# One masked eviction per score tile, a third score buffer and an undeferred unit tail in an attention stage

## The reference

```python
xn = _layernorm(x)
Q, K, V = heads(xn @ Wq + bq), heads(xn @ Wk + bk), heads(xn @ Wv + bv)   # 16 heads of 64
scores = einsum('bhsd,bhtd->bhst', Q, K) / sqrt(64)
mask = where(i - j >= 0, 0.99 ** (i - j), 0.0)          # query i, key j
retained = einsum('bhst,bhtd->bhsd', scores * mask, V)
attn = (layernorm(retained) * gamma + beta) * sigmoid(xn @ Wg + bg) @ Wo + bo
ffn = sum over 8 experts of weight_e * (gelu(xn @ W1_e + b1_e) @ W2_e + b2_e)
out = x + attn + ffn
```

## Time and profile before

| | us |
|---|---|
| runs shown: median of 3 (lowest to highest) | 13451.64 (12078.26 to 13509.96) |
| the profiled execution | 12024.38 |
| its span, slowest core (core 1) | 12022.8 |
| spans of the other seven cores | 12004.4 to 12017.8 |
| mean granted clock by core | 0.843 to 0.849 |

### The profile page before, as it was taken

How to read it: one execution, slowest core, us unless ns; L and a number is a source line. 1 busy time by engine, 2 the same in 40 slices (tenths; PEclk the granted TensorE clock), 3 DMA queues, 4 the chain that set the end, 5 groups by cost and what they waited for, 6 DMA issues and landing times.

```text
span 12022.8 us, 105462 instructions; the slowest of 8 cores (12004.4 to 12022.8 us)
## 1 busy us (share of the span) xinstructions
PE 9491.4 (79%) x39485; PEld 3786.1 (31%) x39485; DVE 5122.3 (43%) x6656; ACT 1631.5 (14%) x1573; POOL 2.3 (0%) x7
## 2 busy tenths in 40 slices
PE   0376762699999999999947776269999999999995
PEld 0111111343343443444411111134444444444442
DVE  4255552344444444444424555334444444444443
ACT  2200001211111111111100000021111111111111
POOL 0000000000000000000000000000000000000000
PEclk7655556899999999999976555579999999999997
DMA  1100001122222222222220000111112211111112
GB/s 42 32 7 7 6 7 27 56 70 70 70 70 70 70 70 71 70 71 70 70 70 8 7 7 7 28 42 70 71 63 77 71 70 70 71 70 70 71 70 70
DMA packets 334567, 636.28 MB, mean 53 GB/s; under 512 B 75460, under 2 KB 125164, under 8 KB 334070
## 3 DMA queue, kind: packets, MB, share of 16 engines
q1 hardware_dynamic: 319862, 578.94, 14.2%
q10 hardware_dynamic: 14208, 50.60, 1.2%
HBM read 612.72 MB, written 16.78 MB: 52 GB/s over the span
## 4 chain that ended last, share of the span: by engine, by line
PE 72%; DVE 12%; DMA 7%; issue 4%; ACT 4%; DVEq 1%; ACTq 0%; SPq 0%
PE ps_h L1304 30%; PE ps_o L1353 29%; PE ps_s L717 4%; PE ps_r L768 3%; DVE st_buf L746 2%; DVE st_buf L751 2%; ACT L1330 1%; ACT hb L1330 1%; PE ps_qk L683 1%; DMA wqk_st<-wk 1%; DVE st_buf L757 1%; PE ps_g L1062 1%; PE ps_v L539 1%; PE ps_o L1136 1%; DMA xo<-x 1%
## 5 line engine op out<-in xcount | busy, mean ns | idle before, releaser
L1376 DVE SCALAR_TENSOR_TENSOR acc<-ps_o,wrt,acc 128x1024 f16<-128x1024 f32 x2048 | 2628.9, 1284 | 4036.3 <-PE ps_o L1353 3963.5
L1304 PE MATMUL ps_h<-xn_t,w1c 128*128 128x512 bf16 x16384 | 3640.3, 385 | 379.8 <-ACT hb L1330 332.3
L1353 PE MATMUL ps_o<-w2c,hb 128*128 128x512 bf16 x16384 | 3601.2, 378 | 8.0 <-DVE acc L1376 5.1
L1304 PEld LDWEIGHTS ps_h<-xn_t,w1c 128*128 128x128 bf16 x16384 | 1613.0, 99 | 2401.1 <-issue 548.1
L1353 PEld LDWEIGHTS ps_o<-w2c,hb 128*128 128x128 bf16 x16384 | 1475.6, 97 | 2111.0 <-issue 590.5
L1330 ACT ACTIVATE hb<-ps_h,b1t 128x1024 bf16<-128x1024 f32 x1024 | 1127.1, 1113 | 1918.6 <-PE ps_h L1304 1917.1
L717 PE MATMUL ps_s<-qp,kp 64*128 64x512 bf16 x1280 | 756.4, 593 | 457.7 <-DVE st_buf L746 198.6
L768 PE MATMUL ps_r<-st_buf,Vt 128*64 128x512 bf16 x1280 | 805.2, 629 | 56.5 <-DVE st_buf L746 54.8
L1330 ACT ACT_TABLE_LOAD x128 | 164.2, 1283 | 4427.0 <-PE ps_o L1353 4291.6
L736 DVE TENSOR_SCALAR st_buf<-ps_s,ckcols 128x512 bf16<-128x512 f32 x768 | 576.3, 750 | 193.6 <-PE ps_s L717 161.0
L717 PEld LDWEIGHTS ps_s<-qp,kp 64*128 64x128 bf16 x1280 | 127.5, 100 | 1028.7 <-issue 1028.7
(11 more groups left out here) (118 smaller groups left out, 2037.2 us busy)
## 6 DMA issues: line engine op xcount, KB each, us to landing
stg<-w SPq DMA_DIRECT2D x256, 2048.0 KB
xin<-x ACTq DMA_DIRECT2D x8, 2048.0 KB, 8.1
xo<-x ACTq DMA_DIRECT2D x32, 512.0 KB, 3.7
out<-oo ACTq DMA_DIRECT2D x32, 512.0 KB, 2.7
stgv<-wv SPq DMA_DIRECT2D x16, 512.0 KB
wqk_st<-wq SPq DMA_DIRECT2D x64, 128.0 KB
wqk_st<-wk SPq DMA_DIRECT2D x64, 128.0 KB
stg<-wg SPq DMA_DIRECT2D x32, 256.0 KB
```

What stands on the lines that cost most here:

```text
L1304: CT.tick(t.matmul(ps_h[hpar][:, n2 * 512:(n2 + 1) * 512], w1c[par][:, dc * 512 + jt * 128: dc * 512 + (jt + 1) * 128], xn_t[:, dc * T + t ...
L1353: CT.tick(t.matmul(ps_o2[opar][:, n2 * 512:(n2 + 1) * 512], hb[:, jt * S + tt * 128: jt * S + (tt + 1) * 128], w2c[par][:, jt * D + n2 * 5 ...
L1376: CV.tick(v.scalar_tensor_tensor(acc[:, tt * D:(tt + 1) * D], ps_o2[opar][:], wrt[:, (b * NTB + tt) * 8 + e: (b * NTB + tt) * 8 + e + 1], ...
```

## The change

The mask of a band block is made once, at the kernel's start: bmask holds for each of the four positions bp in the band a 128x512 tile of zeros, the triangle and ones, written by 16 small DVE instructions. The eviction of a band block becomes one scalar_tensor_tensor over 128x512 that multiplies by ckcols and by bmask. ps_s has three buffers in place of two and S(jt) waits for the eviction of jt-3. ps_ret has one buffer in place of two. The tail is no longer held back: the last AV comes on PE right behind AV(njt-2), and RET on DVE behind the unit's last eviction. bmask takes 4 KB more of each SBUF partition.

```diff
+    bmask = sb("bmask", [128, 4 * 512], BF16)
...
+            for bp in range(4):
+                for isub in range(4):
+                    dst = bmask[:, bp * 512 + isub * 128: bp * 512 + (isub + 1) * 128]
+                    W.w(v, "v", CV, CV.n)
+                    if isub < bp:
+                        CV.tick(v.memset(dst, 0.0))
+                    elif isub == bp:
+                        CV.tick(v.tensor_copy(dst, tri_bf[:]))
+                    else:
+                        CV.tick(v.memset(dst, 1.0))
...
-                            for i in range(2)]
+                            for i in range(3)]
                     ps_ret = [s1.enter_context(u_ps(f"ps_r{i}", [64, IC], F32))
-                              for i in range(2)]
+                              for i in range(1)]
...
-                                        spar = jt % 2
+                                        spar = jt % 3
                                         W.w(t, "t", CV,
-                                            sev[jt - 2] if jt >= 2 else sev_last[spar])
+                                            sev[jt - 3] if jt >= 3 else sev_last[spar])
...
-                                            for sub in range(IC // 128):
-                                                isg = band0 + sub
-                                                d0 = dst0 + sub * 128
-                                                pslice = ps_s[spar][:, sub * 128:(sub + 1) * 128]
...
+                                            bp = jt - band0
+                                            CV.tick(v.scalar_tensor_tensor(
+                                                st_buf[:, dst0:dst0 + IC],
+                                                ps_s[spar][:], ckc,
+                                                bmask[:, bp * 512:(bp + 1) * 512],
+                                                ALU.mult, ALU.mult))
...
-                                            W.w(t, "t", CV, ret_ev[rpar])
+                                            W.w(t, "t", CV, ret_ev[0])
...
-                                if av_pend[0] is not None:
-                                    av_pend[0]()
-                                    av_pend[0] = None
-                                if njt > 1:
                                     EV_sec(0)
...
+                                AV_sec(njt - 1)
...
+                                @block.vector
+                                def _(v, hp=hp, po=po, ic=ic, av_last=av_last):
+                                    W.w(v, "v", CT, av_last)
+                                    W.w(v, "v", CV, CV.n)
+                                    CV.tick(v.tensor_copy(
+                                        retained[po:po + 64,
+                                                 hp * S + ic * IC: hp * S + (ic + 1) * IC],
+                                        ps_ret[0][:]))
+                                    ret_ev[0] = CV.n
```

More of the change, by code:

```diff
@@ L606, in build_program @@
                     kev = [0] * HP
-                    sev_last = list(sev_init)
+                    sev_last = sev_init + [0]
                     slot_av = [0, 0, 0]
-                    av_pend = [None]
                     ret_ev = [0, 0]
@@ L733, in _ @@
                                         ckc = ckcols[:, jt:jt + 1]
+                                        W.w(v, "v", CV, CV.n)
                                         if jt < band0:
-                                            W.w(v, "v", CV, CV.n)
                                             CV.tick(v.tensor_scalar(
@@ L766, in _ @@
                                         if jt == 0:
-                                            W.w(t, "t", CV, ret_ev[rpar])
+                                            W.w(t, "t", CV, ret_ev[0])
                                         CT.tick(t.matmul(
-                                            ps_ret[rpar][:],
+                                            ps_ret[0][:],
                                             Vt[:, jt * D + hgl * 64: jt * D + hgl * 64 + 64],
@@ L791, in build_program @@
                                     EV_sec(0)
-                                for jt in range(njt - 1):
+                                AV_sec(njt - 1)
+                                for jt in range(njt):
                                     slot_av[jt % 3] = max(slot_av[jt % 3], avt[jt])
@@ L796, in build_program @@
                                     sev_last[jt % 2] = max(sev_last[jt % 2], sev[jt])
[L798 to L815, removed]
+                                av_last = avt[njt - 1]
+                                @block.vector
+                                def _(v, hp=hp, po=po, ic=ic, av_last=av_last):
+                                    W.w(v, "v", CT, av_last)
+                                    W.w(v, "v", CV, CV.n)
+                                    CV.tick(v.tensor_copy(
[3 more added lines that the diff above has]
+                                    ret_ev[0] = CV.n
                                 u_idx += 1
-                    if av_pend[0] is not None:
-                        av_pend[0]()
-                        av_pend[0] = None
                     a1_done_v = CV.n
```

## The result

| | before | changed |
|---|---|---|
| ten runs each: median (lowest to highest) | 12550.62 (12034.31 to 13509.96) | 12420.46 (11580.46 to 12927.1) |
| ratio, changed to before | | 0.9624, 95% interval 0.947 to 0.978 |
| the profiled execution: span, slowest core | 12022.8 | 11741.4 |
| spans of its cores | 12004.4 to 12022.8 | 11559.1 to 11741.4 |

The ratio is that of the forecast (11,567 / 12,024 = 0.962), though it rests on few executions, and its interval nearly reaches 0.98, within which a change can't be told from none. The lowest time, 11,580.46, lies 13 us off the forecast.

What follows compares the result with a forecast made beforehand. PE was taken to bind below the diagonal, DVE in the band and at seams. Saving 14.44 us a head gives 462 over 32 heads, 457 after 5 us of losses: 11,567 from 12,024; range 11,480 to 11,720, 80%.

Steps and rivals of the forecast that it cites:

- the sum: Head stages: unit times from last AV to last AV, 45.17 us a head against 59.61, 457 us less in all.
- the range: Whole execution: 11,480 to 11,720 us, meant to hold 8 in 10.
- the experts as long as before: Expert stages: a sign of the forecast, their time unchanged, as the edit has none of their code.
- The masked 128x512 eviction: Band on DVE: 0.75 us each, four replacing 10 narrow multiplies and 6 memsets; bounds 0.35 and 2.35.
- the seam: Between units: last eviction to next first eviction 1.67 us against 2.24; AV0 1.84 after the last AV, PE idle 0.2.
- The units: A head's four units, last AV to last AV: 5.00, 8.99, 13.39 and 17.79 us, DVE binding the first.
- The first eviction of a pair: Start of a pair: 0.71 us from the end of kp, against 2.68 with the held tail, gaining 1.97.
- bmask's writes: Kernel start: 16 writes, 5.3 us, hidden under the 13.64 us wait for the last constant; uncovered, 5 us once.
- The third buffer: Score buffers: lets S2 start at a seam, where PE then idles 0.2 us; buys nothing within a unit.
- the undeferred tail: Rival at the seam: its 1.67 us also holds PE, 214 us come back, 11,781; 6%.
- the buffers without effect: Rival: buffers and order do nothing, only the band counts; PE idles 1.84 us at a seam, 11,777; 3%.
- The clock did not rise: Rival in the head stages: PE's clock rises or stays up, DVE binds throughout, 11,386; 8%.

Runs made afterwards that it cites:

- e11_pair7: e7_pair with the second head's evictions below the diagonal on ACT (Identity, column scale) and seven score buffers; full-clock cores 11229 to 11246 us, ratio to before 0.9305.
- e6_group2: The changed kernel with a unit's matmuls in twos (S, S, AV, AV in place of S, AV, S, AV); full-clock cores 11466 to 11477 us.
- e2_order: The changed kernel with the narrow band evictions put back, so only the order and the buffers change; full-clock cores 11906 to 11931 us.
- e4_held: The changed kernel with the tail held back again behind the next unit's S0 and S1, three score buffers; full-clock cores 11680 to 11703 us.
- e1_band: The kernel before with only the masked 128x512 eviction and bmask; full-clock cores 11731 to 11754 us.
- e7_pair: The changed kernel with a pair's two heads worked together and the band's columns above the diagonal left out; full-clock cores 11203 to 11228 us, ratio to before 0.931.
- e12_pair_act: e11_pair7 with all ACT evictions of a head stage in one section of ACT's program; full-clock cores 10881 to 10908 us.

## Why the prediction was right, and where it was wrong

**The step that failed is the last one,** from the sum to the range. I made the sum against one execution's 12,024 and bounded it by terms of the head stage alone, 11,480 to 11,720. The expert stages stood in it as a constant ("the experts as long as before"). They are not: of the ten executions only the one at 11,580 is inside the range. The runs of before, 12,078 to 13,510, were in front of me and said so, and I put them aside in a sentence. The missing term was PE's clock in the expert stages: 172 us of matmul time on core 1 of the profiled execution. The longest of the ten, 12,927, has no trace; its long cores have mean clocks of 0.752 to 0.769 against 0.858 on a core of 11,558. A trace of such an execution is there for e11_pair7, whose expert code is the same. Its core 1 spans 12,419.2 us, its core 5 11,229.0, and the experts of core 1 read:

```profile
L1304 PE MATMUL ps_h<-xn_t,w1c 128*128 128x512 bf16 x16384 | 4249.4, 430 | 380.1 <-ACT hb L1330 332.3 <-DVE w1c L1262 47.9
L1353 PE MATMUL ps_o<-w2c,hb 128*128 128x512 bf16 x16384 | 4120.4, 420 | 5.1 <-ACT hb L1330 2.9 <-DVE acc L1376 2.2
```

That is 8370 us, against 7243 on core 5: 1127 of the 1190 between the two, with a clock of 0.80 against 0.99 from 8400 to 9400 us. A range for the median had to reach over what the runs of before spread. Which cores are hit, and why, stays open.

The Trainium skill (TensorE: Matmul & The Clock Gate, Part 1) tells of a peak-current limiter that lowers the clock of a whole die when three of its cores run dense matmuls. In the profiled execution the lowering comes by pairs: cores 0, 1, 4 and 5 are longer (11,682 to 11,741), and 2, 3, 6 and 7, on the same two dies and in the same stages, are not (11,559 to 11,573). In others of the ten a whole die is longer (12,637 to 12,779 on cores 4 to 7) and the other, with the same work, is not (11,556 to 11,580). So dense matmuls on all eight cores don't always bring the lower clock here, and the measurement doesn't fit the rule as it stands.

**The terms of the sum held.**

- The masked 128x512 eviction was put at 0.75 and took 0.750.
- At the seam AV0 was put 1.84 behind the end of the last AV and came 1.86 behind it (643.73 to 645.59). PE was said to idle 0.2 of that and idles 0.47: S0, S1 and S2 in a row take 1.46, not 3 x 0.55, as no change of shape lies between them (e6_group2). The sum does not feel it, since DVE's chain sets AV0.
- The units were put at 5.00, 8.99, 13.39 and 17.79 and took 5.02, 9.08, 13.48 and 17.88. The 0.09 more in a long unit is 9 us over 32 heads.
- The first eviction of a pair was put 0.71 behind kp; it starts 0.70 after it (kp ends at 724.21, the eviction starts at 724.91).
- bmask's writes were put at 5.3 us under a wait. They take 5.2 and do lie there, and what is left of the wait of 13.64 is 7.85:

```profile
4.30 0.20 DVE L249 COPY bmask<-tri_bf 128x128 bf16<-128x128 bf16 x1
...
9.46 0.17 DVE L253 MEMSET ones_r<- 1x128 bf16 x1
...
17.68 0.19 DVE L258 CAST wr_bf<-wr_st 128x64 bf16<-128x64 f32 x1 [7.85 <-DMA b_row<-b]
```

- The two head stages together were put 457 us shorter; at the end of the second one core 1 is 451 ahead.
- The third buffer was said to buy time at the seam only; taking it away cost 57 us, 57 expected.

Cores at the full clock so end at 11,556 to 11,595, around the 11,567 of the sum.

One reading in the prediction was off: 11,781 for the undeferred tail and 11,777 for the buffers without effect are a hair more than 2% below 12,024, not within it, so the two rivals should have counted as faster. The forecast does not hang on it.

**The rivals.** The clock did not rise. The table by stretches of core 2 has PE busy for 10.00 of 10.00 us at a clock of 0.50:

```profile
655.00:665.00 10.00, 10.00 (x19) 1.99 (x18) 7.36 (x10) 0.00 (x0) 0.00 (x0) 0.50 0.00 0
```

The undeferred tail did not cost its chain (e2_order, e4_held). The wide multiply was not dear (0.750). The buffers and the order did something (e2_order to e4_held).

## What to carry to other kernels

When two limits alternate, write the recurrence from durations and gaps of the trace and run it through a whole unit, seam included; it gave seven of the variants here (e1_band to e7_pair) to within 25 us of 12,000. It missed the three with ACT in them by some 290, 190 and 85 us, where table loads and a higher clock were not in the terms. A tail that is held back to hide it is worth a look at what it then stands behind: here two matmuls and a shared buffer. And take the spread of the runs shown into the range before any term of your own; a stage that the edit doesn't touch can move more than the one it does.

One thing in the changed kernel should not be copied: S takes its buffer by jt % 3, while sev_last, which holds what S of a new unit has to wait for, is still kept by jt % 2, so the third buffer's entry is never brought up to date. Here this does no harm, as the unit's last AV, ahead of the next S0 on PE, has waited for the last eviction. With a tail held back it could, and e4_held has jt % 3 in both.

## What the hardware showed that I had not expected

- A matmul of 64 rows next to one of the other 64 rows costs nothing extra: two S took 0.61 together in e11_pair7 at a clock of 0.50, where two S of the same rows took 1.03 in e6_group2.
- Alternating S and AV cost 0.12 us for each change of shape (1.10 a block against 0.98 in e6_group2).
- Each section of ACT's program that was read begins with a table load of 1.28 us, with Copy as with Identity: 192 in a stage in e11_pair7, one in e12_pair_act.
- With S and AV filling half the array each, PE busy for 10.00 of 10.00 us stayed at 0.50, the 1.2 GHz level. In e12_pair_act core 7 has a mean granted clock of 0.73 over the first 550 us of the stage, projections included, and PE is busy for 378 us of them:

```profile
600.00:1150.00 550.00, 378.43 (x1511) 122.68 (x1509) 313.85 (x482) 111.54 (x169) 0.00 (x0) 0.73 0.04 12
```

In e7_pair, core 6, the same stretch is at 0.57, with PE busy for more of it:

```profile
600.00:1150.00 550.00, 416.69 (x1213) 110.23 (x1212) 349.35 (x520) 0.00 (x0) 0.00 (x0) 0.57 0.03 10
```

The other cores of e12_pair_act have 0.64 to 0.73 there. So the stretch with the shorter busy time has the higher clock. A higher clock itself shortens the busy time, the two kernels differ in more than one thing, and no run takes them apart: why the clock rose stays open.
